# An attention block on one core: the input by tokens and the output through 32x32 squares instead of TensorE transposes

## The chip, the cores and the metric

One core of one Trainium2 chip runs the kernel. The metric is the device time of one execution in microseconds (us); lower is better.

## The reference

The input `x` has 16 batches of 256 channels and 32 x 32 positions, all in 32-bit floats. A batch is 1024 tokens of 256 channels. What is computed, batch by batch:

```python
xn = group_norm(x, 8 groups) * norm_w + norm_b
q, k, v = qkv_w @ xn + qkv_b
x1 = x + proj_w @ (softmax(q.T k / 16) v) + proj_b      # first attention, residual
t = tokens(x1)                                          # [1024, 256]
n = layer_norm(t); c = n / |n|
t = t + softmax((c c.T) ** 2) @ n                       # second attention
l = layer_norm(t)
y = (l @ (sign(w - mean(w)) * mean|w|)) + bias
t = t + round(clip(y, -1, 1) * 7) / 7                   # quantised feed-forward
out = t turned back to [256, 32, 32]
```

## The kernel before, in words

Each engine has a program written out by hand, and semaphores tie them together. A number is split into a high and a low part, and each product takes three matmuls (low by high, high by low, high by high). The weights are folded once at the start: queries and keys into one matrix, values and projection into another.

A batch has a `front` and a `back` (TensorE L532 and L604, ScalarE L724 and L764, VectorE L972 and L1031, GpSimd L1170). The front of batch b also finishes batch f = b - 1. On TensorE the order of the front is: transpose the first half of `x_raw` into `turn` (`x_by_tokens`, L372, 8 transposes of 128x128), queries 0 (12 matmuls of 512 columns), the second half of `x_raw`, queries 1, transposes of the second norm of batch f (`turn_ln2`, L507), values, the feed-forward product (`ffn`, L515, 8 matmuls of 512 columns for a half), and the transposes of `tok` of batch f (`turn_t`, L525, 8 for a half), which bring the tokens into the layout of the output. Two score blocks (`scores1`, L405) go between these. Then come steps s = 1 to 8: a score block, the transposes of the exponentials (`turn_e1`, L429) and the product with the values of the block before (`product1`, L437). After step 1 a product waits until VectorE has read the result before it out of the shared bank: `product1(b, 1)` waits for `t1_made` of `residual1(b, 0)`. Then follow the second scores (L455), and in the back the second product (L484).

VectorE works strictly in its written order: `x_tokens` (L873) adds the bias to the transposed `x` and writes `x_tok`, which `residual1` (L898) adds; `row_max` (L889), `e1T_lo` (L894, the low part of the exponentials), `gn_sums` (L851, statistics of the next batch), `clip` (L953), and `output` (L966), which adds the quantised result to the transposed `tok` in PSUM. ScalarE applies scale and bias of the feed-forward (`ffn_out`, L716), and GpSimd rounds (L1161). SyncE issues the DMAs: two loads of 512 KB for a batch (L281), once the transposes have read `x_raw` and it is normalised, and two stores of 512 KB (L285), whose runs in memory are 2 KB. The last batch runs the same steps from other PSUM banks (`LAST`, L261).

Of the kernel before, what the change touches and what calls it, by code (L numbers as in the profile page):

```python
# [30 lines left out]
ALU = mybir.AluOpType  # L31
# [4 lines left out]
BANK = 512  # L36
GROUPS = 8
# [7 lines left out]
def build(nc, x, norm_w, norm_b, qkv_w, qkv_b, proj_w, proj_b, ffn_w, ffn_b, out):  # L45
# [11 lines left out]
    assert KC == 2 and N == 2 * BANK and C // GROUPS == 32  # L57
    scale = float(C) ** -0.5

    x_d = x.rearrange("b (k p) h w -> b p k (h w)", p=P)  # L60
    out_d = out.rearrange("b (k p) h w -> b p k (h w)", p=P)

    with ExitStack() as ctx:
# [25 lines left out]
        out_bias = sb("out_bias", [P, C])  # L89
        norm_w_c = sb("norm_w_c", [P, KC])  # L90
        norm_b_c = sb("norm_b_c", [P, KC])
        ffn_b_c = sb("ffn_b_c", [P, KC])
# [8 lines left out]
        xn_lo = sb("xn_lo", [P, KC, N], F32R)  # L101
        x_tok = sb("x_tok", [P, NT, C])
# [8 lines left out]
        y_sb = sb("y_sb", [P, 2, KC, HALF])  # L111
# [52 lines left out]
        bv_wide = expo[:, 1, 0:KC * P].rearrange("p (t c) -> p t c", c=P)  # L164
        abs_w = x_tok[:, 0:KC, :]

# [28 lines left out]
        xT_up = sem("xT_up")  # L195
# [53 lines left out]
        tT_up = sem("tT_up")  # L249
        out_made = sem("out_made")  # L250
        stored = [sem("stored0"), sem("stored1")]

        QKV_LOADS, NORM_LOADS, FFN_LOADS = 16 * 3, 16 * 2, 16 * 3
# [6 lines left out]
        PLACES = dict(ln2T=[turn, turn], y=y_wide, tT=[turn, turn])  # L260
        LAST = dict(ln2T=[turn, wide[1]], y=[y_wide[0], [narrow[0][:, :], narrow[1][:, :]]], tT=[turn, wide[1]])  # L261
# [16 lines left out]
        def _(sp):  # L278
# [4 lines left out]
            def store(f, hf):  # L283
                sp.wait_ge(out_made, 2 * f + hf + 1)
                sp.dma_start(out_d[f, :, :, hf * HALF:(hf + 1) * HALF], y_sb[:, hf]).then_inc(stored[hf], 16)  # L285

            load_x(0)
            with nc.allow_non_contiguous_dma("columns of biases, once"):
# [6 lines left out]
                sp.dma_start(ffn_b_c[:, :], ffn_b.rearrange("(k p) -> p k", p=P)).then_inc(ffn_loaded, 16)  # L295
# [935 lines left out]
```

## Time and profile before

| | |
|---|---|
| Median of 3 runs | 1854.93 us (1854.73 to 1854.97) |
| The profiled execution | 1856.45 us |
| Its span, first to last instruction | 1854.7 us |
| Mean granted clock of TensorE | 0.998 |
| TensorE busy | 99% |
| VectorE, ScalarE, GpSimd busy | 68%, 49%, 52% |
| Read from memory, written to it | 18.23 MB, 16.78 MB |

All durations below are of the profiled execution, which took 1.75 us more than its span and 1.52 us more than the median. Batches repeat: the first turn of `x` of one batch starts at 1265.93 us, and the batch after it runs in the same order some 114 us later. Times in the rows are counted from the start of the span. A matmul's duration in a row includes its passage through the array, so the pace of TensorE is read from one start to the next.

### The profile page before, as it was taken

To read this page: it belongs to the slowest core of one execution; us is meant where nothing else is said; L and a number is where in the kernel's file an instruction comes from. 1 tells how busy PE (TensorE), PEld (TensorE's weight loads), DVE (VectorE), ACT (ScalarE), POOL (GpSimd) and SP (SyncE) were. 2 spreads that over 40 slices of the span, in tenths; PEclk is the share of its full clock that TensorE was granted. 3 is DMA by queue.
4 is the path that set the end of the run, shared out by engine and by line. 5 is a ranking of instruction groups with operands and counts; after the bars stand their busy time and mean duration, and the time that the engine had idled before them with its cause. 6 is when DMAs were issued, how large, how long until landed. Compare 5 with 4: busy or idle time off the path is not lost.

```text
span 1854.7 us, 36871 instructions
## 1 busy us (share of the span) xinstructions
PE 1835.7 (99%) x12834; PEld 1699.1 (92%) x12834; DVE 1268.1 (68%) x2516; ACT 906.7 (49%) x1444; POOL 959.6 (52%) x2262
## 2 busy tenths in 40 slices
PE   7999999999999999999999999999999999999997
PEld 6999999989899998999989999999998999989997
DVE  6676766767666676666767667676676766767566
ACT  3545546445463544635446354454544536355452
POOL 0654727457274472734737356372654727447272
PEclk9999999999999999999999999999999999999999
DMA  2000010000100001000010100001000010000000
GB/s 77 1 24 24 1 45 0 23 23 0 45 0 23 23 0 45 0 34 11 0 45 0 45 0 10 35 0 45 0 23 23 0 45 0 23 23 0 24 1 23
DMA packets 16415, 35.42 MB, mean 19 GB/s; under 512 B 2688, under 2 KB 4096, under 8 KB 16384
## 3 DMA queue, kind: packets, MB, share of 16 engines
q1 hardware_dynamic: 16384, 35.01, 5.2%
q8 instruction: 19, 0.31, 0.1%
q14 instruction: 12, 0.10, 0.0%
HBM read 18.23 MB, written 16.78 MB: 19 GB/s over the span
## 4 chain that ended last, share of the span: by engine, by line
PE 98%; DVE 0%; DMA 0%; ACT 0%; SPq 0%; issue 0%; POOL 0%; ACTq 0%; POOLq 0%; DVEq 0%
PE wide L322 35%; PE narrow L424 8%; PE narrow L426 8%; PE narrow L425 8%; PE turn L434 6%; PE wide L424 5%; PE wide L426 5%; PE wide L425 5%; PE narrow L322 5%; PE wide L520 3%; PE turn L481 3%; PE turn L377 2%; PE narrow L452 2%; PE turn L511 1%; PE turn L528 1%; DMA qkv_b_c<-in_L_conv_qkv_b 0%
## 5 line engine op out<-in xcount | busy, mean ns | idle before, releaser
L322 PE MATMUL wide<-xn_hi,prob 128*128 128x512 f32 x1024 | 310.1, 404 | 0.0
L676 ACT ACTIVATE prob<-turn 128x1024 fp32r<-128x1024 f32 x128 | 131.3, 1026 | 322.0 <-PE turn L434 322.0
L1109 POOL TENSOR_TENSOR ln_v<-ln_mv,ln_eps 128x1 f32<-128x1 f32 x256 | 49.3, 193 | 428.8 <-DVE ln_mv L909 251.7
L891 DVE TENSOR_REDUCE neg_max<-wide 128x1 f32<-128x1024 f32 x128 | 156.4, 1222 | 123.0 <-PE wide L322 123.0
L690 ACT ACTIVATE ln<-tok,ln_shift,ln_r 128x256 f32<-128x256 f32 x128 | 77.2, 603 | 319.7 <-POOL ln_shift L1114 319.7
L424 PE MATMUL narrow<-prob 128*128 128x256 f32 x768 | 225.0, 293 | 0.0
L426 PE MATMUL narrow<-prob 128*128 128x256 f32 x768 | 217.0, 283 | 0.0
L425 PE MATMUL narrow<-prob 128*128 128x256 f32 x768 | 216.9, 282 | 0.0
L322 PEld LDWEIGHTS wide<-xn_hi,prob 128*128 128x128 f32 x1024 | 182.8, 188 | 35.4
L896 DVE TENSOR_TENSOR prob<-turn,prob 128x1024 fp32r<-128x1024 f32 x128 | 156.7, 1224 | 61.8 <-ACT prob L676 61.8
L669 ACT ACTIVATE expo<-wide,neg_max 128x1024 f32<-128x1024 f32 x128 | 142.5, 1113 | 58.2 <-DVE neg_max L891 58.1
L322 PE MATMUL wide<-xn_lo,prob 128*128 128x512 f32 x512 | 160.7, 395 | 0.0
L1149 POOL TENSOR_TENSOR prob<-expo,prob 128x128 fp32r<-128x128 f32 (+6 forms) x112 | 150.3, 1358 | 9.0 <-DVE prob L919 9.0
L424 PE MATMUL narrow<-val,prob 128*128 128x258 f32 x512 | 148.6, 290 | 0.0
L425 PEld LDWEIGHTS narrow<-prob 128*128 128x128 f32 x768 | 147.1, 191 | 0.0
L424 PE MATMUL wide<-val,prob 128*128 128x258 f32 x512 | 146.9, 287 | 0.0
L424 PEld LDWEIGHTS narrow<-prob 128*128 128x128 f32 x768 | 146.9, 191 | 0.0
L426 PEld LDWEIGHTS narrow<-prob 128*128 128x128 f32 x768 | 146.7, 191 | 0.0
L1138 POOL TENSOR_TENSOR cos_x<-ln_x,len_i 128x256 f32<-128x256 f32 x128 | 78.7, 615 | 130.7 <-ACT ln_x L683 126.6
L426 PE MATMUL wide<-val,prob 128*128 128x258 f32 x512 | 145.0, 283 | 0.0
L426 PE MATMUL narrow<-val,prob 128*128 128x258 f32 x512 | 145.0, 283 | 0.0
L425 PE MATMUL wide<-val,prob 128*128 128x256 f32 x512 | 144.6, 282 | 0.0
(171 smaller groups left out, 5479.1 us busy)
## 6 DMA issues: line engine op xcount, KB each, us to landing
x_raw<-in_x SPq DMA_DIRECT2D x32, 512.0 KB, 3.9
out<-y_sb SPq DMA_DIRECT2D x32, 512.0 KB, 2.8
tok<-in_L_conv_qkv_w SPq DMA_DIRECT2D x1, 768.0 KB, 6.8
ln<-in_L_conv_proj_w SPq DMA_DIRECT2D x1, 256.0 KB, 6.8
ln<-in_L_ffn_weight SPq DMA_DIRECT2D x1, 256.0 KB, 3.0
out_bias<-in_L_conv_proj_b SPq DMA_DIRECT2D x1, 128.0 KB, 3.8
qkv_b_c<-in_L_conv_qkv_b SPq DMA_DIRECT2D x1, 3.0 KB, 7.4
norm_w_c<-in_L_conv_norm_w SPq DMA_DIRECT2D x1, 1.0 KB, 6.1
```

Source lines behind the costliest of these rows:

```text
L322: mm = pe.matmul(o, lhsT, r, start=first and i == 0, stop=last and i == len(parts) - 1)
L424: pe.matmul(o[:, 0:w], hi, value_hi(j), start=j == 0, stop=False)
L425: pe.matmul(o[:, 0:C], hi, value_lo(j), start=False, stop=False, skip_group_check=True)
L426: mm = pe.matmul(o[:, 0:w], lo, value_hi(j), start=False, stop=j == NT - 1)
L434: mm = pe.transpose(turn[:, tile(j)], expo[:, n % DEEP, tile(j)], ident[:, :])
L669: act.activation(expo[:, n % DEEP], wide[n % 2][:, :], ACT.Exp, bias=neg_max[:, n:n + 1], accum_out=row_sum1[:, n:n + 1]).then_inc(e1_made, 1)
L676: act.activation(eT_hi[:, n % 2], turn[:, :], ACT.Copy).then_inc(eT_hi_made, 1)
L690: act.activation(ln2[:, n], tok[:, n], ACT.Identity, bias=ln2_shift[:, n:n + 1], scale=ln2_r[:, n:n + 1]).then_inc(ln2_made, 1)
L891: dve.tensor_reduce(neg_max[:, n:n + 1], wide[n % 2][:, :], AX.X, ALU.max, negate=True).then_inc(max_made, 1)
L896: dve.tensor_sub(eT_lo[:, n % 2], turn[:, :], eT_hi[:, n % 2].bitcast(F32)).then_inc(eT_made, 1)
L1138: pool.tensor_tensor(cos_x[:, r], ln_x[:, r], len_i[:, n:n + 1].broadcast_to([P, C]), ALU.mult).then_inc(cos_made, 1)
L1149: pool.tensor_sub(prob[:, 1, J, row], expo[:, J % DEEP, row], prob[:, 0, J, row].bitcast(F32)).then_inc(p_made, 1)
```

## The change

The token layout of `x` is no longer made on TensorE. `x` is loaded a second time, in 32 DMAs for a batch (4 groups of 32 partitions by 8 channel blocks), each of 256 runs of 128 bytes, so that every 32x32 square lies in one group of 32 partitions (`x_quad`). ScalarE adds the bias to it in place, in 8 instructions of 256 elements (`bias_quad`), which stand between the instructions of `layer_norm2` of the batch before. VectorE turns the squares, in two instructions of 1024 elements (`x_tokens`), which stand in steps 0 and 2 of the front.

The feed-forward product is made with tokens on the partitions (16 matmuls of 256 columns for a half), and its scale and bias move from ScalarE to VectorE (`ffn_out`, one instruction of 1024 elements for a half). `output` stands in steps 1 and 4 now. It adds `tok` to the quantised result, both in SBUF, and turns the squares of the sum into `out_quad`, which lies in the memory of `ln2`. SyncE stores it in 32 DMAs for a batch, again of 128-byte runs, and the first `layer_norm2` of the next batch waits until all 32 have landed. `x_by_tokens` and `turn_t` are gone. The last batch is added by tokens, turned on TensorE (`turn_last`), copied out by ScalarE and VectorE, and stored in two DMAs with 2 KB runs.

The first load of the squares stands behind the loads of the weights. In the loop SyncE issues, in this order: the two loads of `x_raw` of batch b + 1, the 32 loads of squares of batch b + 1 once `x_tokens` of batch b is done, and the 32 stores of batch b - 1 once its second `output` is done.

```diff
     x_d = x.rearrange("b (k p) h w -> b p k (h w)", p=P)
+    xq_d = x.rearrange("b (cb cc) (n tq) w -> b tq cc cb n w", cc=Q, tq=P // Q)
+    outq_d = out.rearrange("b (cb cc) (n tq) w -> b tq cc cb n w", cc=Q, tq=P // Q)
     out_d = out.rearrange("b (k p) h w -> b p k (h w)", p=P)
...
+        quad_bias = sb("quad_bias", [P, C // Q, Q])
...
-        ffn_b_c = sb("ffn_b_c", [P, KC])
+        ffn_bias = sb("ffn_bias", [P, C])
...
+        x_quad = sb("x_quad", [P, C // Q, NT, Q])
...
-        y_sb = sb("y_sb", [P, 2, KC, HALF])
+        y_sb = sb("y_sb", [P, 2, HT, C])
...
+        out_last = expo[:, 0:2, :].rearrange("p h (k t) -> p h k t", k=KC)
         abs_w = x_tok[:, 0:KC, :]
+        out_quad = ln2[:, :, :].rearrange("p t c -> p (t c)").rearrange("p (cb n tt) -> p cb n tt", cb=C // Q, n=NT)
...
-        PLACES = dict(ln2T=[turn, turn], y=y_wide, tT=[turn, turn])
-        LAST = dict(ln2T=[turn, wide[1]], y=[y_wide[0], [narrow[0][:, :], narrow[1][:, :]]], tT=[turn, wide[1]])
+        PLACES = dict(ln2T=[turn, turn], y=y_wide)
+        LAST = dict(ln2T=[turn, wide[1]], sum=[turn, wide[1]], y=[y_wide[0], [narrow[0][:, :], narrow[1][:, :]]])
...
-            def store(f, hf):
-                sp.wait_ge(out_made, 2 * f + hf + 1)
-                sp.dma_start(out_d[f, :, :, hf * HALF:(hf + 1) * HALF], y_sb[:, hf]).then_inc(stored[hf], 16)
+            def load_quads(b):
+                for tq in range(P // Q):
+                    for cb in range(C // Q):
+                        sp.dma_start(x_quad[tq * Q:(tq + 1) * Q, cb], xq_d[b, tq, :, cb]).then_inc(quad_loaded, 16)
+            def store(f):
+                sp.wait_ge(out_made, 2 * f + 2)
+                for tq in range(P // Q):
+                    for cb in range(C // Q):
+                        sp.dma_start(outq_d[f, tq, :, cb], out_quad[tq * Q:(tq + 1) * Q, cb]).then_inc(stored, 16)
+            def store_last(hf):
+                sp.wait_ge(last_made[hf], 2)
+                sp.dma_start(out_d[B - 1, :, :, hf * HALF:(hf + 1) * HALF], out_last[:, hf]).then_inc(last_stored, 16)
...
+            load_quads(0)

             def reload(b):
-                sp.wait_ge(xT_up, 2 * b)
                 sp.wait_ge(xn_made, 2 * b)
                 load_x(b)

+            def reload_quads(b):
+                sp.wait_ge(xT_made, 2 * b)
+                load_quads(b)
             reload(1)
+            reload_quads(1)
             with sp.Fori(1, B - 1) as b:
                 reload(b + 1)
-                store(b - 1, 0)
-                store(b - 1, 1)
-            for f in (B - 2, B - 1):
-                store(f, 0)
-                store(f, 1)
-            sp.wait_ge(stored[0], 16 * B)
-            sp.wait_ge(stored[1], 16 * B)
+                reload_quads(b + 1)
+                store(b - 1)
+            store(B - 2)
+            for hf in range(2):
+                store_last(hf)
+            sp.wait_ge(stored, 16 * QUADS * (B - 1))
+            sp.wait_ge(last_stored, 32)
...
-            def x_by_tokens(b, g):
-                if g:
-                    pe.wait_ge(xT_made, 2 * b + 1)
-                for t in range(HT):
-                    for k in range(KC):
-                        mm = pe.transpose(turn[:, t * C + k * P:t * C + (k + 1) * P],
-                                          x_raw[:, k, tile(HT * g + t)], ident[:, :])
-                mm.then_inc(xT_up, 1)
...
             def ffn(f, hf, places=PLACES):
                 pe.wait_ge(ln2T_made, 2 * f + hf + 1)
-                for m in range(KC):
+                for t in range(HT):
+                    o = places["y"][hf][t // 2][:, t % 2 * C:(t % 2 + 1) * C]
                     for k in range(KC):
                         for part in (tokT_lo, tokT_hi):
-                            mm = pe.matmul(places["y"][hf][m], sign_w[:, k, tile(m)],
-                                           part[:, k, hf * HALF:(hf + 1) * HALF],
+                            mm = pe.matmul(o, part[:, k, tile(HT * hf + t)], sign_w[:, k, :],
                                            start=k == 0 and part is tokT_lo, stop=k == KC - 1 and part is tokT_hi)
                 mm.then_inc(y_up, 1)

-            def turn_t(f, hf, places=PLACES):
+            def turn_last(hf):
+                pe.wait_ge(sum_made, 2 * (B - 1) + hf + 1)
                 for k in range(KC):
                     for t in range(HT):
-                        mm = pe.transpose(places["tT"][hf][:, k * HALF + t * P:k * HALF + (t + 1) * P],
-                                          tok[:, HT * hf + t, tile(k)], ident[:, :])
-                mm.then_inc(tT_up, 1)
+                        mm = pe.transpose(LAST["sum"][hf][:, k * HALF + t * P:k * HALF + (t + 1) * P],
+                                          y_sb[:, hf, t, tile(k)], ident[:, :])
+                mm.then_inc(last_up, 1)
...
                     pe.wait_ge(x_loaded[k], 16 * b + 16)
                 if f is not None:
-                    pe.wait_ge(pT_made, (NT - 1) * f + NT - 1)
-                x_by_tokens(b, 0)
-                if f is not None:
                     pe.wait_ge(t2_made, NT * f + NT - 1)
                 queries(b, 0)
-                x_by_tokens(b, 1)
                 if f is not None:
                     pe.wait_ge(t2_made, NT * f + NT)
                 else:
                     pe.wait_ge(prep_dve, 8)
                 queries(b, 1)
                 if f is not None:
-                    pe.wait_ge(xT_made, 2 * b + 2)
...
+                    pe.wait_ge(pT_made, (NT - 1) * f + NT - 1)
                     turn_ln2(f, 0)
...
-                    turn_t(f, 0)
-                    pe.wait_ge(y_made, 4 * f + 2)
+                    pe.wait_ge(y_made, 2 * f + 1)
                 scores1(b, 0)
                 if f is not None:
-                    pe.wait_ge(out_made, 2 * f + 1)
-                    turn_t(f, 1)
-                    pe.wait_ge(y_made, 4 * f + 4)
+                    pe.wait_ge(y_made, 2 * f + 2)
                 scores1(b, 1)
-                if f is not None:
-                    pe.wait_ge(out_made, 2 * f + 2)
-                else:
-                    pe.wait_ge(xT_made, 2 * b + 2)
                 turn_e1(b, 0)
...
-            turn_t(f, 0, LAST)
             turn_ln2(f, 1, LAST)
             ffn(f, 1, LAST)
-            turn_t(f, 1, LAST)
+            for hf in range(2):
+                turn_last(hf)
...
+            def bias_quad(b, cb):
+                if cb == 0:
+                    act.wait_ge(quad_loaded, 16 * QUADS * (b + 1))
+                mm = act.activation(x_quad[:, cb], x_quad[:, cb], ACT.Identity, bias=quad_bias[:, cb, 0:1])
+                if cb == C // Q - 1:
+                    mm.then_inc(quad_biased, 1)
+            def layer_norm2(b, n, again=True):
                 act.wait_ge(ln2_scale, NT * b + n + 1)
+                if again and n == 0:
+                    act.wait_ge(stored, 16 * QUADS * b)
                 act.activation(ln2[:, n], tok[:, n], ACT.Identity, bias=ln2_shift[:, n:n + 1],
                                scale=ln2_r[:, n:n + 1]).then_inc(ln2_made, 1)
...
-            def ffn_out(f, hf, reuse, places=PLACES):
-                act.wait_ge(y_up, 2 * f + hf + 1)
-                if reuse:
-                    act.wait_ge(stored[hf], 16 * f)
-                for m in range(KC):
-                    act.activation(y_sb[:, hf, m], places["y"][hf][m], ACT.Identity,
-                                   bias=ffn_b_c[:, m:m + 1], scale=w_mean[:, 1:2]).then_inc(y_made, 1)
...
+                if f is None:
+                    act.wait_ge(quad_bias_made, 1)
+                    for cb in range(C // Q):
+                        bias_quad(0, cb)
...
                 for n in range(NT):
-                    layer_norm2(b, n)
+                    layer_norm2(b, n, again)
+                    if more:
+                        bias_quad(b + 1, n)
...
+                act.wait_ge(last_up, hf + 1)
+                act.activation(out_last[:, hf, 0], LAST["sum"][hf][:, 0:HALF], ACT.Copy).then_inc(last_made[hf], 1)
...
             def x_tokens(b, g):
-                dve.wait_ge(xT_up, 2 * b + g + 1)
-                dve.tensor_tensor(x_tok[:, HT * g:HT * (g + 1), :],
-                                  turn[:, :].rearrange("p (t c) -> p t c", t=HT),
-                                  out_bias[:, :].unsqueeze(1).broadcast_to([P, HT, C]), ALU.add).then_inc(xT_made, 1)
+                dve.wait_ge(quad_biased, b + 1)
+                dve.transpose(x_tok[:, HT * g:HT * (g + 1), :].rearrange("p n (cb cc) -> p n cb cc", cc=Q),
+                              x_quad[:, :, HT * g:HT * (g + 1), :].rearrange("p cb n tt -> p n cb tt")
+                              ).then_inc(xT_made, 1)
...
+            def ffn_out(f, hf, places=PLACES):
+                dve.wait_ge(y_up, 2 * f + hf + 1)
+                wholes = [wide[hf][:, :]] if places is PLACES else places["y"][hf]
+                step = HT // len(wholes)
+                for i, whole in enumerate(wholes):
+                    last = dve.scalar_tensor_tensor(
+                        y_sb[:, hf, i * step:(i + 1) * step], whole.rearrange("p (t c) -> p t c", t=step),
+                        w_mean[:, 1:2], ffn_bias[:, :].unsqueeze(1).broadcast_to([P, step, C]), ALU.mult, ALU.add)
+                last.then_inc(y_made, 1)
...
-            def output(f, hf, places=PLACES):
-                dve.wait_ge(tT_up, 2 * f + hf + 1)
+            def add_tokens(f, hf):
                 dve.wait_ge(q_made, 2 * f + hf + 1)
-                dve.tensor_tensor(y_sb[:, hf], places["tT"][hf][:, :].rearrange("p (k t) -> p k t", k=KC), y_sb[:, hf],
-                                  ALU.add).then_inc(out_made, 1)
+                dve.tensor_tensor(y_sb[:, hf], tok[:, HT * hf:HT * (hf + 1)], y_sb[:, hf], ALU.add).then_inc(sum_made, 1)
+            def output(f, hf):
+                add_tokens(f, hf)
+                dve.wait_ge(ln2T_up, 2 * f + 2)
+                dve.wait_ge(sum_made, 2 * f + hf + 1)
+                dve.transpose(out_quad[:, :, HT * hf:HT * (hf + 1)].rearrange("p cb n tt -> p n cb tt"),
+                              y_sb[:, hf].rearrange("p n (cb cc) -> p n cb cc", cc=Q)).then_inc(out_made, 1)
...
-                x_tokens(b, 0)
-                if f is None:
+                    dve.transpose(quad_bias[:, :, :], out_bias[:, :].rearrange("p (cb cc) -> p cb cc", cc=Q)
+                                  ).then_inc(quad_bias_made, 1)
                     signs()
-                x_tokens(b, 1)
...
+                    ffn_out(f, 0)
                     clip(f, 0)
...
+                    ffn_out(f, 1)
                     clip(f, 1)
...
-                    output(f, 0)
                 row_max(b, 0)
-                if f is not None:
-                    output(f, 1)
                 row_max(b, 1)
                 e1T_lo(b, 0)
+                x_tokens(b, 0)
                 if more:
                     gn_sums(b + 1, 0)
...
+                    if s == 2:
+                        x_tokens(b, 1)
+                    if f is not None and s in (1, 4):
+                        output(f, s // 4)
...
+            ffn_out(f, 0, LAST)
             clip(f, 0)
             ln2T_lo(f, 1, LAST)
             quantise(f, 0)
-            output(f, 0, LAST)
+            ffn_out(f, 1, LAST)
             clip(f, 1)
+            add_tokens(f, 0)
             quantise(f, 1)
-            output(f, 1, LAST)
+            add_tokens(f, 1)
+            for hf in range(2):
+                dve.wait_ge(last_up, hf + 1)
+                dve.tensor_copy(out_last[:, hf, 1], LAST["sum"][hf][:, HALF:N]).then_inc(last_made[hf], 1)
```

## Rows read from the trace of the kernel before

**Rows 1.** The page, parts 1 and 4: engine TensorE, and the chain by engine.

```profile
PE 1835.7 (99%) x12834; PEld 1699.1 (92%) x12834; DVE 1268.1 (68%) x2516; ACT 906.7 (49%) x1444; POOL 959.6 (52%) x2262
...
PE 98%; DVE 0%; DMA 0%; ACT 0%; SPq 0%; issue 0%; POOL 0%; ACTq 0%; POOLq 0%; DVEq 0%
```

**Rows 2.** Timeline of TensorE, start of a batch: start us, length us.

```profile
1265.93 1.03 PE L377 MATMUL turn<-ident,x_raw 128*128 128x128 f32 x8
1266.72 0.72 PE L322 MATMUL wide<-xn_hi,qk_lo 128*128 128x512 f32 x2
...
1269.61 1.03 PE L377 MATMUL turn<-ident,x_raw 128*128 128x128 f32 x8
...
1276.95 0.42 PE L520 MATMUL wide<-tokT_lo,sign_w 128*128 128x512 f32 x1
```

**Rows 3.** Timeline of TensorE, steps 1 and 2 of the same batch.

```profile
1299.15 0.64 PE L322 MATMUL wide<-xn_hi,prob 128*128 128x512 f32 x2
...
1301.95 1.04 PE L434 MATMUL turn<-ident,expo 128*128 128x128 f32 x8
1302.75 0.36 PE L424 MATMUL narrow<-prob 128*128 128x256 f32 x1
...
1305.70 0.28 PE L364 MATMUL narrow<-gn_mv,group_mean 128*128 128x2 f32 x2
```

**Rows 4.** Timeline of VectorE, where it splits the turned second norm.

```profile
1275.54 1.22 DVE L950 TENSOR_TENSOR tokT_lo<-turn,tokT_hi 128x1024 fp32r<-128x1024 f32 x1 [2.44 <-ACT tokT_hi L712]
```

**Rows 5.** Timeline of three engines after the first score block.

```profile
1288.06 1.03 PE L528 MATMUL turn<-ident,tok 128*128 128x128 f32 x8
...
1288.26 1.23 DVE L891 TENSOR_REDUCE neg_max<-wide 128x1 f32<-128x1024 f32 x1 [0.36 <-PE wide L322]
...
1290.53 0.19 ACT L669 ACTIVATION_READ_ACCUMULATOR expo<-wide,neg_max 128x1 f32 x1
```

**Rows 6.** Timeline of VectorE from the first split of exponentials to the first residual.

```profile
1293.87 1.23 DVE L896 TENSOR_TENSOR prob<-turn,prob 128x1024 fp32r<-128x1024 f32 x1 [0.70 <-ACT prob L676]
1295.01 1.28 DVE L854 BATCH_NORM_STATS2 gn_stats<-x_raw 128x6 f32<-128x512 f32 x2
...
1300.28 0.48 DVE L904 SCALAR_TENSOR_TENSOR tok<-narrow,inv_sum,x_tok 128x256 f32<-128x256 f32 x1
```

**Rows 7.** Groups of VectorE, shapes kept apart.

```profile
L924 DVE TENSOR_TENSOR prob<-expo,prob 128x512 fp32r<-128x512 f32 x32 | 82.1, 2567 | 1.1
...
L875 DVE TENSOR_TENSOR x_tok<-turn,out_bias 128x1024 f32<-128x1024 f32 x32 | 39.2, 1224 | 30.7 <-PE turn L377 30.5
...
L955 DVE TENSOR_SCALAR y_sb<-y_sb 128x1024 f32<-128x1024 f32 x32 | 22.2, 694 | 34.8 <-ACT y_sb L721 33.1
```

**Rows 8.** Groups of ScalarE, shapes kept apart.

```profile
L690 ACT ACTIVATE ln<-tok,ln_shift,ln_r 128x256 f32<-128x256 f32 x128 | 77.2, 603 | 319.7 <-POOL ln_shift L1114 319.7
```

**Rows 9.** Timeline of VectorE and TensorE in steps 4 and 5.

```profile
1317.79 1.23 DVE L896 TENSOR_TENSOR prob<-turn,prob 128x1024 fp32r<-128x1024 f32 x1 [0.37 <-ACT prob L676]
...
1323.23 0.36 PE L424 MATMUL narrow<-prob 128*128 128x256 f32 x1
```

**Rows 10.** Timeline of the SyncE queue: two loads issued.

```profile
1270.81 0.92 SPq L281 DMA_DIRECT2D x_raw<-in_x  x2
```

**Rows 11.** The page, part 3: the DMA queue of loads and stores.

```profile
q1 hardware_dynamic: 16384, 35.01, 5.2%
```

**Rows 12.** DMA view of 9.2 to 10.0 us, where bias columns load.

```profile
DMA packets 506, 0.11 MB, mean 134 GB/s; under 512 B 403, under 2 KB 506, under 8 KB 506
```

**Rows 13.** Timeline of ScalarE where the back of the batch begins.

```profile
1356.60 2.00 ACT L652 ACTIVATE xn_hi<-x_norm 128x1024 fp32r<-128x1024 f32 x2
```

**Rows 14.** Timeline at the end, TensorE and VectorE.

```profile
1843.46 0.50 PE L520 MATMUL narrow<-tokT_lo,sign_w 128*128 128x512 f32 x1 [2.41 <-DVE tokT_lo L950]
...
1850.23 1.22 DVE L969 TENSOR_TENSOR y_sb<-wide,y_sb 128x1024 f32<-128x1024 f32 x1
```

**Rows 15.** Windows, one stretch: busy of PE, PEld, DVE, ACT, POOL; clock; DMA.

```profile
1844.50:1847.50 3.00, 3.00 (x11) 2.46 (x10) 1.46 (x2) 1.01 (x2) 0.00 (x0) 0.50 0.17 66
```

More of the change, by code:

```diff
@@ L36 @@
 BANK = 512
+Q = 32
 GROUPS = 8
@@ L56, in build @@
     NP = len(PARTS)
-    assert KC == 2 and N == 2 * BANK and C // GROUPS == 32
+    assert KC == 2 and N == 2 * BANK and C // GROUPS == 32 and W == Q
     scale = float(C) ** -0.5
     x_d = x.rearrange("b (k p) h w -> b p k (h w)", p=P)
+    xq_d = x.rearrange("b (cb cc) (n tq) w -> b tq cc cb n w", cc=Q, tq=P // Q)
+    outq_d = out.rearrange("b (cb cc) (n tq) w -> b tq cc cb n w", cc=Q, tq=P // Q)
     out_d = out.rearrange("b (k p) h w -> b p k (h w)", p=P)
@@ L194, in build @@
         xn_lo_made = sem("xn_lo_made")
-        xT_up = sem("xT_up")
+        quad_loaded = sem("quad_loaded")
+        quad_bias_made = sem("quad_bias_made")
+        quad_biased = sem("quad_biased")
         xT_made = sem("xT_made")
@@ L248, in build @@
         q_made = sem("q_made")
-        tT_up = sem("tT_up")
+        sum_made = sem("sum_made")
         out_made = sem("out_made")
-        stored = [sem("stored0"), sem("stored1")]
+        stored = sem("stored")
+        last_up = sem("last_up")
+        last_made = [sem("last_made0"), sem("last_made1")]
+        last_stored = sem("last_stored")
+        QUADS = (P // Q) * (C // Q)
         QKV_LOADS, NORM_LOADS, FFN_LOADS = 16 * 3, 16 * 2, 16 * 3
@@ L714, in ln2T_hi, with front @@
                                ).then_inc(ln2T_hi_made, 1)
-            def ffn_out(f, hf, reuse, places=PLACES):
-                act.wait_ge(y_up, 2 * f + hf + 1)
-                if reuse:
-                    act.wait_ge(stored[hf], 16 * f)
-                for m in range(KC):
-                    act.activation(y_sb[:, hf, m], places["y"][hf][m], ACT.Identity,
-                                   bias=ffn_b_c[:, m:m + 1], scale=w_mean[:, 1:2]).then_inc(y_made, 1)
-            def front(b, f, more, reuse=True):
+            def front(b, f, more):
                 query_hi(b, 0)
@@ L732, in front @@
                     ln2T_hi(f, 1)
-                    ffn_out(f, 0, reuse)
                 value_hi(b, 2)
                 value_hi(b, 3)
-                if f is not None:
-                    ffn_out(f, 1, reuse)
+                if f is None:
+                    act.wait_ge(quad_bias_made, 1)
+                    for cb in range(C // Q):
+                        bias_quad(0, cb)
                 exp1(b, 0)
@@ L762, in front, with back @@
                         layer_norm1(b, NT - 1)
-            def back(b, more):
+            def back(b, more, again=True):
                 if more:
@@ L780, in _ @@
             front(0, None, True)
-            back(0, True)
-            front(1, 0, True, reuse=False)
+            back(0, True, again=False)
+            front(1, 0, True)
             with act.Fori(2, B - 1) as b:
@@ L793, in _ @@
                 layer_norm2(f, n)
-            ffn_out(f, 0, True, LAST)
             ln2T_hi(f, 1, LAST)
-            ffn_out(f, 1, True, LAST)
+            for hf in range(2):
+                act.wait_ge(last_up, hf + 1)
+                act.activation(out_last[:, hf, 0], LAST["sum"][hf][:, 0:HALF], ACT.Copy).then_inc(last_made[hf], 1)
         @block.vector
@@ L990, in front @@
                 if f is not None:
+                    ffn_out(f, 1)
                     clip(f, 1)
-                    output(f, 0)
                 row_max(b, 0)
-                if f is not None:
-                    output(f, 1)
                 row_max(b, 1)
                 e1T_lo(b, 0)
+                x_tokens(b, 0)
                 if more:
@@ L1058, in _ @@
             quantise(f, 0)
-            output(f, 0, LAST)
+            ffn_out(f, 1, LAST)
             clip(f, 1)
+            add_tokens(f, 0)
             quantise(f, 1)
-            output(f, 1, LAST)
+            add_tokens(f, 1)
+            for hf in range(2):
+                dve.wait_ge(last_up, hf + 1)
+                dve.tensor_copy(out_last[:, hf, 1], LAST["sum"][hf][:, HALF:N]).then_inc(last_made[hf], 1)
         @block.gpsimd
```

6 lines of the change are left out of this document (3 added, 3 removed).

## The prediction

> **What bounds the kernel now.** First the page: TensorE is busy 99% of the span, and the chain that ended last runs through it for 98% [rows 1]. So the first question is what leaves TensorE, and the second which wait opens once it has less to do. A busy time of matmuls includes their passage through the array, so I take the pace from starts in the timeline [rows 2, 3]. Then I read VectorE's timeline beside it, where the new instructions go [rows 6], and the places where one engine hands over to another with little to spare [rows 4, 5, 9]. All sums are made against the profiled execution of 1856.45 us, which is 1.52 us above the median; the difference is then put to the median of 1854.93 us.
>
> **TensorE loses 3.52 us a batch.** Eight turns of `x` take from 1265.93 to 1266.72, that is 0.79 us [rows 2]. The 12 query matmuls behind them take 2.89 us (1266.72 to 1269.61), while 12 of the same size behind a product take 2.80 us (1299.15 to 1301.95) [rows 2, 3]. So a group of turns is worth 0.79 + 0.09 = 0.88 us. A batch has four of them that go: two of `x`, and two of `tok`, which are the same instructions on another tile. That is 3.52 us, and it occurs in the 15 batches from 1 to 15: 52.8 us. In batch 0 only the two of `x` go, 1.76 us.
>
> The feed-forward product keeps its 4096 columns for a half. By 12 x 512 columns in 2.80 us it takes 1.87 us; by 24 x 256 columns in 2.95 us (1302.75 to 1305.70) [rows 3] it would take 1.97 us. Most of that difference is the slow first matmul behind the turns, which `ffn` hasn't got. I take nothing, and keep 0.2 us a batch (3 us in all) for the range.
>
> **VectorE gives back 1.7 us in 14 batches.** Its order is strict. Between the first split of the exponentials and the first residual it has no idle time: a 1024-element instruction starts at 1293.87 and the next one at 1295.01, so each such one is worth 1.14 us, and the residual that frees the bank ends at 1300.28 + 0.48 = 1300.76 [rows 6]. TensorE starts the product that waits for it (`product1(b, 1)`) at 1302.75 [rows 3]. The slack is 1.99 us, less the handover; one handover from VectorE to TensorE takes at most 0.19 us (an instruction from 1275.54 to 1276.76, the waiting matmul at 1276.95) [rows 2, 4]; at 0.14 us for it, 1.85 us are left. Into this stretch go `x_tokens(b, 0)` and `output(f, 0)`: a turn, an add, and a turn that waits for the add.
>
> - The add has 1024 elements, as L875 has (1224 ns) [rows 7], plus 0.04 us as the turn waits for it: 1.26 us. GpSimd waits for the residual's statistics here, so nothing of it reads SBUF beside.
> - No row shows a 32x32 turn. Below, it might cost what one-source work of 1024 elements in SBUF costs, 694 ns (L955). Above, VectorE is at its slowest where it reads SBUF beside GpSimd: 512 elements in 2567 ns (L924), so 5.13 us for 1024 [rows 7]. I take 1.14 us, the pace of ordinary work on 1024 elements, since GpSimd is idle here.
>
> Together 1.14 + 1.26 + 1.14 = 3.54 us, less 1.85: a stall of 1.7 us at `product1(b, 1)`. It needs both an old output to finish and statistics of the next batch to make: batches 1 to 14, so 14 x 1.7 = 23.8 us. In batch 0 there is no output, and in batch 15 no statistics; the slack holds there.
>
> The Trainium skill (Vector Engine (DVE) Microarchitecture Reference, 3.8) says that the turning array sustains one element per cycle per lane; no run so far shows it. By it the price would be that of the ordinary rows, and the sum the same.
>
> **Step 4.** The second `output` stands behind the split that starts at 1317.79. VectorE is free at 1318.93, and the next product waits until 1323.23 [rows 9]. Less 0.64 us for the reciprocal and the residual and 0.15 for the handover, 3.5 us are open. It needs 1.26 + 1.14 = 2.4 us. GpSimd has two jobs of 256 elements in SBUF then; if the add were contended throughout it would take 5.13 us [rows 7], a stall of 2.8 us. I take one more microsecond, 3.4 us in all, which just fits: no stall.
>
> **The front.** VectorE loses two `x_tokens` (1.22 us each) and two `output` adds, and gains two `ffn_out` of 1024 elements from PSUM, which is L875's form [rows 7]: no more than before. Where the cover shrinks is the first softmax row: TensorE is through with score block 0 at 1288.06, VectorE starts its maximum at 1288.26, and ScalarE has the sum read out at 1290.72 [rows 5]. That is 2.66 us, plus up to 0.19 for the handover. Before, turns and a score block covered it; now only a score block of 2.80 us. It fits by 0.1 us at best and misses by 0.05. The split of the second norm [rows 4] is covered by the values as before. For such near misses I take 0.1 us in each of 15 batches: 1.5 us.
>
> **ScalarE.** The eight `bias_quad` cost 603 ns each by L690, and ScalarE idles 319.7 / 128 = 2.5 us before each of these norms [rows 8]. Cover: the product of the back. In batch 0 there is no such cover: 8 x 0.6 = 4.8 us stand before the first exponential, so of the 1.76 us saved there I keep 0.6 (bounds: all of it, or 3 us lost).
>
> **DMAs.** A batch gets 32 loads and 32 stores, on a queue where two issues take 0.92 us [rows 10]: 64 x 0.46 = 29.4 us. Their runs are 64 x 256 = 16384 packets, 1024 for each of 16 engines. Below, a packet costs 25 ns: 506 in 0.8 us where bias columns load [rows 12]. Above, 94 ns: 5.2% of 16 x 1854.7 us for 16384 packets of 2 and 4 KB or less [rows 11]. So 26 to 96 us. They may start after step 2 (about 1306) and must have landed when the first norm of the back may start, behind the two ScalarE instructions that end at 1358.60 [rows 13]: 52 us. Queued behind that norm are all the others and the next queries' copies. A 128-byte run is nearer to the bias columns, so I take it as hidden; the order of the queue does not delay `x_raw`, which has a whole batch.
>
> The Trainium skill (DMA: Bandwidth & Descriptors, Specifications) speaks against the change: under 512 bytes a transfer falls short of line rate and is read, modified and written. If that were to decide, it is the last rival below; no row shows a 128-byte store.
>
> **The end.** Now the last half is finished by an ending at 1850.23 + 1.22 = 1851.45 [rows 14]. The new order puts behind the last product the other half's add (1.14), a turn (0.79 at full clock, 1.6 at half) and a copy of 512 elements (0.7), with two handovers: 2.9 to 3.7 us more. I take 3.2.
>
> **Sum.** -52.8 - 0.6 + 23.8 + 1.5 + 3.2 = -24.9 us. The profiled execution would take 1831.5 us, the median 1830.0 us. A measurement of this kernel can tell 0.2% (3.7 us) from no change.
>
> **Rivals.**
> 1. *The turn is cheap, or the stall doesn't come.* At 0.65 us a turn the stall is 2.56 - 1.85 = 0.7 us, so 14 us less: 1816; with no stall 1806. For it: L955 works on the same bytes faster. Against: few rows are that fast. 12%.
> 2. *TensorE's clock falls at each stall.* At the end TensorE idles 2.41 us before 1843.46 [rows 14], and then the granted clock is 0.50 for 3 us [rows 15], the lower level of 1.2 GHz. Three microseconds at half lose 1.5 us of work; 14 times is 21 us more: 1851. Against: my stall is shorter than that idle time, with full work on both sides. 12%.
> 3. *Many small handovers come to light.* With TensorE 3.5 us shorter, each 0.04 to 0.3 us of slack may turn out missing; 1 us a batch is 15 us: 1845. 9%.
> 4. *Slower: a turn costs two passes.* Place: the same stall. At a turn of price P it is 2P - 0.6 us a batch, and the change loses from P = 2.1 us on (14 x 3.6 = 50). At 2.3 us it is 4.0 us, 56 in all, and step 4 then misses by 1.1 us, another 16: 24.9 us of gain become 23 of loss, 1878. For it: no row shows this instruction, and L924 shows that work in SBUF can be far dearer. 12%.
> 5. *Slower: the 128-byte runs are late.* Above 51 ns a packet (some 60 with ScalarE's idle time) the first norm waits for the stores and TensorE behind it. At 94 ns they need 96 us and miss by over 35 us in each batch: 2300. 5%.
>
> The forecast has 50%, with 1822 to 1841 as its own range. That the change doesn't do what it says has no chance of its own: every removed turn is in the code of the loop.
>
> **Numbers.** 80% range: from rival 1's middle to past rival 2, 1808 to 1860. Faster by over 0.2% (under 1851.2): 50 + 12 + 9 and half of rival 2, with a little of 4: 78%. Within 0.2%: 6%. Slower: 16%.
>
> **What would show it.** Right: no turn of `x_raw` or `tok` on TensorE; a batch of about 112.2 us instead of 114; one idle time of TensorE of 1.7 us a batch, before the second product of the values, released by the residual; the turns near 1.2 us; the first norm of the back not waiting for a DMA. Wrong: turns of 2 us or more, a granted clock under 1.00 in steps 2 and 3, idle time before the feed-forward or the first turn of exponentials, or ScalarE waiting on `stored` or `quad_loaded`.

## The result: slower, 1930.05 against 1854.92 us

| | before | after |
|---|---|---|
| median of 4 runs, us | 1854.92 (1854.73 to 1854.97) | 1930.05 (1927.35 to 1933.26) |
| ratio, 95% interval | 1 | 1.0406 (1.0388 to 1.0424) |
| profiled execution, span | 1856.45, 1854.7 | 1930.54, 1928.8 |

The forecast was 1830.0 us with a range to 1860; the time is 100 us above it.

The page of the changed kernel, parts 1 and 4 (as [rows 1]), part 3 (the DMA queues) and part 6 (issues):

```profile
PE 1823.0 (95%) x12594; PEld 1692.2 (88%) x12594; DVE 1340.4 (69%) x2583; ACT 916.0 (47%) x1510; POOL 963.8 (50%) x2262
...
q1 hardware_dynamic: 277920, 51.98, 13.9%
q8 instruction: 136, 2.23, 0.5%
...
PE 75%; DVE 8%; issue 7%; POOL 7%; SPq 1%; ACT 1%; POOLq 0%; DMA 0%; DVEq 0%; ACTq 0%
...
x_quad<-in_x SPq DMA_DIRECT2D x512, 32.0 KB, 2.3
out<-ln SPq DMA_DIRECT2D x480, 32.0 KB, 1.9
```

TensorE no longer fills the chain, and "issue" has 7% of it: time in which the engine waited for nothing that the profile shows. One line looked harmless. The instruction queue, q8, brought 136 packets of 16 KB. Before the change it brought 19:

```profile
q8 instruction: 19, 0.31, 0.1%
```

Where does TensorE wait now? Its waits in the changed kernel (engine, line, releaser: us in total, times, longest):

```profile
PE narrow L445 <- issue: 44.4, 18, 3.6
PE narrow L445 <- POOL prob L1189: 21.1, 8, 2.8
PE narrow L445 <- DVE tok L920: 19.5, 14, 1.4
```

The third is the stall that was forecast, 14 times. The other two are 26 idle times, two for each of the 13 times that the loop returns to its head (its body runs 14 times). A turn of the loop is one pass through its body here; the turns of `x` and of the squares are transposes. The timeline of TensorE shows them for one turn, at the first instructions of the loop body, `product2(f, 0)`:

```profile
1293.08 0.82 PE L502 MATMUL turn<-ident,expo 128*128 128x128 f32 x6
1296.61 0.38 PE L445 MATMUL narrow<-val,prob 128*128 128x258 f32 x1 [2.71 <-POOL prob L1189]
...
1297.68 0.34 PE L447 MATMUL narrow<-val,prob 128*128 128x258 f32 x1
1299.86 0.58 PE L445 MATMUL narrow<-val,prob 128*128 128x258 f32 x1 [1.84 <-issue]
```

Nine matmuls run between the two idle times. The clock follows; windows of the same turn, with the granted clock third from the end:

```profile
1297.00:1297.50 0.50, 0.50 (x6) 0.50 (x6) 0.47 (x2) 0.00 (x0) 0.50 (x1) 1.00 0.00 0
...
1297.60:1304.40 6.80, 4.96 (x25) 4.69 (x24) 4.73 (x6) 0.00 (x0) 3.37 (x2) 0.51 0.48 155
```

So for 6.8 us, the second idle time among them, the granted clock is at the lower of its two levels, 1.2 GHz. TensorE is busy for 4.96 us of these, and half of that, about 2.5 us, is lost. With 2.71 + 1.84 us of idle time that is 7.0 us in this turn. A turn of the loop takes 119.41 us (the forecast stall stands at 1240.56 and again at 1359.97).

### The profile page after: what moved, and what is told of

It reads as the page before. It is cut to its first block, busy times and chain, and to the rows that moved or that the text cites. A ratio compares the mean times of both kernels' runs of the same rounds, so it can differ in the third digit from the quotient of the medians.

```text
span 1928.8 us, 39117 instructions
## 1 busy us (share of the span) xinstructions
PE 1823.0 (95%) x12594; PEld 1692.2 (88%) x12594; DVE 1340.4 (69%) x2583; ACT 916.0 (47%) x1510; POOL 963.8 (50%) x2262
## 3 DMA queue, kind: packets, MB, share of 16 engines
q1 hardware_dynamic: 277920, 51.98, 13.9%
## 4 chain that ended last, share of the span: by engine, by line
PE 75%; DVE 8%; issue 7%; POOL 7%; SPq 1%; ACT 1%; POOLq 0%; DMA 0%; DVEq 0%; ACTq 0%
PE wide L352 22%; PE narrow L445 8%; PE narrow L447 8%; PE narrow L446 8%; POOL prob L1189 5%; PE wide L445 5%; PE wide L447 5%; PE wide L446 5%; PE turn L455 5%; PE narrow L352 4%; PE wide L542 3%; DVE gn_stats L870 2%; PE turn L532 1%; SPq L299 1%; PE turn L502 1%
## 5 line engine op out<-in xcount | busy, mean ns | idle before, releaser
L352 PE MATMUL wide<-xn_hi,prob 128*128 128x512 f32 x1024 | 305.3, 402 | 0.0
L445 PE MATMUL narrow<-val,prob 128*128 128x258 f32 x512 | 162.8, 318 | 65.5 <-issue 44.4
L445 PEld LDWEIGHTS narrow<-val,prob 128*128 128x128 f32 x512 | 111.0, 217 | 72.2 <-issue 48.9
L445 PEld LDWEIGHTS narrow<-prob 128*128 128x128 f32 x768 | 146.7, 191 | 22.8 <-DVE tok L920 22.8
L447 PE MATMUL narrow<-val,prob 128*128 128x258 f32 x512 | 158.1, 309 | 0.0
L446 PE MATMUL narrow<-val,prob 128*128 128x256 f32 x512 | 157.9, 308 | 0.0
L1189 POOL TENSOR_TENSOR prob<-expo,prob 128x128 fp32r<-128x128 f32 (+6 forms) x112 | 149.9, 1354 | 9.0 <-DVE prob L935 9.0
```

What stands on the lines that cost most here:

```text
L352: mm = pe.matmul(o, lhsT, r, start=first and i == 0, stop=last and i == len(parts) - 1)
L445: pe.matmul(o[:, 0:w], hi, value_hi(j), start=j == 0, stop=False)
L446: pe.matmul(o[:, 0:C], hi, value_lo(j), start=False, stop=False, skip_group_check=True)
L447: mm = pe.matmul(o[:, 0:w], lo, value_hi(j), start=False, stop=j == NT - 1)
L1189: pool.tensor_sub(prob[:, 1, J, row], expo[:, J % DEEP, row], prob[:, 0, J, row].bitcast(F32)).then_inc(p_made, 1)
```

## The experiments

Three theories were set against each other. **A, the instruction fetch:** TensorE's code comes from memory in blocks, packets of 16 KB on q8. While the body of the loop is resident (all of it held by the engine), a turn fetches nothing; now the body lies differently against these blocks, and is fetched anew in every turn. **B, the traffic:** the 64 transfers of 128-byte runs per batch delay the fetches or push code out. **C, the engines:** VectorE's new work makes GpSimd's `e2_lo` late, as the releaser "POOL prob L1189" suggests.

TensorE's program was counted for this, a matmul as two instructions (weight load and multiply). Ahead of the loop the changed kernel has 33 fewer than before (16 turns of `x` in batch 0, and a wait); the body has 1658, against 1693. A block is taken as 256 instructions; idle78 and idle82 test that.

**idle17, idle100: the body moved.** Idle transposes go where TensorE has nothing to do; their result is overwritten:

```diff
             pe.wait_ge(consts_made, 3)
+            for _ in range(17):
+                pe.transpose(turn[:, 0:P], ident[:, :], ident[:, :])
             group_means(0)
```

> This is the kernel after the change, with 17 transposes of the identity (34 instructions for TensorE) added ahead of its first group mean, where TensorE has nothing to do before 7 us. They restore nearly the number of TensorE instructions (1187 against 1154) that stood ahead of the loop before the change. Theory A (the instruction fetch: in the changed kernel TensorE's loop body lies so against the 16 KB blocks in which its code is fetched that it no longer stays resident, and every turn of the loop fetches it again): the 16 KB fetches fall from 136 to about 20, none of them in the loop after its first pass; the two stalls of TensorE at the start of product 2 (about 2.7 and 1.9 us) and the stretch at clock 0.50 behind them go; time 1815 to 1836 us. Theory B (the 64 transfers of 128-byte runs per batch delay the fetches): nothing changes, 1928 to 1933 us, 136 fetches. Theory C (VectorE's added work makes GpSimd's e2_lo late at product 2): nothing changes, 1928 to 1933 us.

Measured: 1832.85 us (1832.47 to 1833.31), ratio to before 0.9869 (0.9853 to 0.9886). 34 instructions that compute nothing save 97 us. The instruction queue has 19 packets again. The waits of TensorE in idle17, the first two:

```profile
PE narrow L445 <- DVE tok L922: 19.5, 14, 1.4
PE turn L550 <- DVE y_sb L996: 3.4, 1, 3.4
```

The DMA view from 1230 to 1700 us, a stretch with four heads of the body. First the changed kernel, nine fetches a turn, then idle17, where the two are of the code behind the loop:

```profile
q8 instruction: 36, 0.59, 0.5%
```

```profile
q8 instruction: 2, 0.03, 0.0%
```

Traffic, engines and their order are unchanged, and both kinds of stall are gone, also the one named after GpSimd. B and C fall for this kernel; A stands.

> The kernel after the change with 100 such idle transposes (200 instructions) instead of 17: a control for the idle transposes themselves. Theory A: the place of the loop against the blocks is what counts and not the number of idle transposes; 200 instructions move it on into a place where the body (some 1658 instructions, 6.5 blocks of 256) again touches 8 blocks: about 130 fetches, 1920 to 1940 us. If instead any idle work at the start helps, 1815 to 1836 us. Theories B and C: 1928 to 1935 us.

Measured: 1880.65 us (1870.34 to 1890.04), 92 fetches. Slower than idle17 by 48 us and faster than expected. Some 6 us of this lie ahead of the loop: the first forecast stall ends at 166.05 us, against 160.33 in idle17. The trace has 8 idle times of 2.4 to 4.3 us at the head of the body, and so 5 turns of 13 without one. The waits of TensorE:

```profile
PE narrow L445 <- issue: 23.7, 6, 4.3
...
PE narrow L445 <- POOL prob L1191: 5.1, 2, 2.6
```

So it isn't idle work that helps. But the expectation of 1920 us and more missed: with 8 blocks touched, a turn may still be spared.

**before60: the same illness in the old kernel.** The same edit with 60 transposes, in the kernel before.

> The kernel before the change with 60 idle transposes (120 instructions) ahead of TensorE's first group mean and nothing else. Theory A: its loop body (1693 instructions, 6.6 blocks) is moved onto 8 blocks, and the old kernel gets the same illness: 110 to 140 fetches instead of 19, a stall of some 3 to 5 us at the start of product 2 and a stretch at clock 0.50 each turn, 1930 to 1975 us. Theories B and C: 1855 to 1857 us, since neither the transfers nor VectorE are touched.

Measured: 1906.59 us (1904.29 to 1915.1), ratio 1.0281 (1.0256 to 1.0306), 137 fetches. The trace shows one idle time in each turn, for instance:

```profile
1273.54 0.82 PE L481 MATMUL turn<-ident,expo 128*128 128x128 f32 x6
1277.17 0.38 PE L424 MATMUL narrow<-val,prob 128*128 128x258 f32 x1 [2.81 <-issue]
1277.39 0.28 PE L425 MATMUL narrow<-val,prob 128*128 128x256 f32 x1
```

The cause doesn't need the change. The price is below the expected one: 50 us, 3.8 per turn, since there is one idle time a turn and the clock falls in only 7 of 13.

**beforequads: the traffic alone.** In the kernel before, on SP's queue:

```diff
             with sp.Fori(1, B - 1) as b:
                 reload(b + 1)
+                sp.wait_ge(xT_made, 2 * b + 2)
+                sp.wait_ge(quad_loaded, 16 * 32 * (2 * b - 1))
+                load_quads(b + 1)
                 store(b - 1, 0)
                 store(b - 1, 1)
+                sp.wait_ge(quad_loaded, 16 * 32 * (2 * b))
+                load_quads(b + 1)
```

> The kernel before the change with 64 loads of 128-byte runs per loop turn added on SP's queue (the quad loads of x, twice), into a buffer that nothing reads; TensorE's and VectorE's code is untouched. Theory B (this traffic delays the instruction fetches or throws the code out): stalls at the start of product 2 and over 100 fetches of 16 KB, 1900 to 1940 us. Theory A: 19 to 25 fetches and 1854 to 1860 us; so too theory C.

Measured: 1856.29 us, ratio 0.9995 (0.9986 to 1.0005), with all the packets:

```profile
q1 hardware_dynamic: 268800, 65.48, 15.9%
q8 instruction: 19, 0.31, 0.1%
```

B falls here too. The added transfers were loads; 128-byte stores were not added to the kernel before. They run in idle17, though, as in the changed kernel, and there nothing is fetched again.

**idle60, idle8: the same number in the other kernel, and a smaller one.** The edit of idle17 with 60 and with 8.

> The kernel after the change with the same 60 idle transposes (120 instructions) that made the kernel before slower by 50 us. By the instruction fetch the shorter body (1658 against 1693 instructions) still fits onto 7 blocks of 256 there: 1832 to 1835 us and about 19 fetches of 16 KB. If what counts is only whether there are few or many idle transposes, or if idle work at the start does harm by itself, it is slow like idle100 and before60: over 1870 us.

Measured: 1834.88 us (1832.95 to 1836.1), 20 fetches. The 60 transposes that cost the kernel before 50 us take 95 us off the changed one.

> The kernel after the change with only 8 idle transposes (16 instructions). The body then begins 16 instructions further on. If its last instructions just reach into an eighth block in the changed kernel, a few are enough: 1831 to 1836 us; if 16 are too few, still over 1900 us and more than 100 fetches. Either way it places the edge between 0 and 34 instructions.

Measured: 1936.71 us (2 runs), 136 fetches. The edge lies between 15 and 33 instructions. The timeline places it better. Here three matmuls run between the two idle times, where the changed kernel has nine:

```profile
1297.91 0.38 PE L445 MATMUL narrow<-val,prob 128*128 128x258 f32 x1 [2.65 <-POOL prob L1191]
1298.13 0.28 PE L446 MATMUL narrow<-val,prob 128*128 128x256 f32 x1
1298.25 0.28 PE L447 MATMUL narrow<-val,prob 128*128 128x258 f32 x1
1300.93 0.58 PE L445 MATMUL narrow<-val,prob 128*128 128x258 f32 x1 [2.39 <-issue]
```

Six matmuls fewer, with a register instruction for every three, are 14 instructions, and the body was moved by 15. So the second idle time stands at a fixed place in the code, the end of a block, some 25 instructions into the changed kernel's body. The next four runs test it.

**idle12, idle14, idle78, idle82: both edges.**

> The kernel after the change with 12 idle transposes. In its trace TensorE stops for the second time behind the 9th matmul of the loop body, and in idle8 (15 instructions more ahead of the body, since one wait melts into another instruction) behind the 3rd: by the program's order a block of code ends there, some 25 instructions into the body of the changed kernel. 12 idle transposes move the body on by 23 instructions, so it still begins one to three before the end of a block and touches 8: over 1900 us, more than 100 fetches. If the edge isn't where the blocks say, 1831 to 1837 us.

Measured: 1943.71 us (2 runs), 136 fetches. The two idle times have become one:

```profile
1305.01 0.58 PE L445 MATMUL narrow<-val,prob 128*128 128x258 f32 x1 [6.05 <-issue]
```

> The kernel after the change with 14 idle transposes, 4 instructions more than idle12: the body is moved on by 27 and begins just inside the next block, so it touches 7. 1831 to 1837 us and 19 or 20 fetches, no stall at the start of product 2. If the blocks are not the cause, the same as idle12.

Measured: 1831.92 us (1831.89 to 1831.94), 19 fetches. **Two transposes, four instructions of some 5000, are worth 112 us.** The edge lies between 23 and 27 instructions.

> The other edge. With 78 idle transposes (155 instructions) the body begins some 130 instructions into its first block; 130 + 1658 is 1788, less than 7 blocks of 256 (1792): 1831 to 1838 us and about 20 fetches.

Measured: 1837.88 us (1836.86 to 1838.89), 20 fetches, no such stall. It is 6 us above idle14, and all of that lies ahead of the loop, where the long row of idle transposes ends late: the first forecast stall ends at 165.78 us, against 159.72 in idle14, and the last at 1626.10 against 1619.81.

> 8 instructions more than idle78: 138 + 1658 is 1796, over 7 blocks of 256. The last few instructions of the body reach into an eighth block: at least some turns of the loop fetch again, over 1860 us and over 60 fetches. If seven blocks are not the limit, the same as idle78.

Measured: 1856.74 us (8 runs, 1851.95 to 1863.87), 56 fetches; it was expected above 1860 with over 60. The side of the edge is right, the price too high: in the profiled execution only four turns stall, by 4.0 to 4.2 us:

```profile
PE narrow L445 <- issue: 16.2, 4, 4.2
```

With idle100 it shows two kinds of bad place. Where the body begins just ahead of a block's end (idle8, idle12, the changed kernel) every turn fetches 9 blocks. Where its last instructions reach into an eighth block, only some turns do. before60 is of the second kind by its place, and yet fetched in every turn; why, no run shows.

**split17: the forecast stall tested.** On top of idle17:

```diff
+                    if f is not None and s == 1:
+                        add_tokens(f, 0)
-                    if f is not None and s in (1, 4):
-                        output(f, s // 4)
+                    if f is not None and s in (3, 5):
+                        output(f, s // 4, add=s == 5)
```

> The kernel after the change with the 17 idle transposes, and VectorE's first output in two pieces: the add stays in step 1 (the first residual overwrites what it reads), its turn goes from step 1 to step 3; the second output goes whole from step 4 to step 5. If the 1.39 us stall at product 1 of each batch is the price of VectorE's added work ahead of the first residual, one turn (1.25 us) less leaves 0 to 0.2 us of it: 14 x 1.2 = 17 us off 1832.85, 1813 to 1820 us, with no fetches in the loop. If the stall has another cause, or only moves to a later product, 1828 to 1836 us.

Measured: 1814.01 us (1813.75 to 1815.29), ratio 0.9769 (0.9756 to 0.9782). The listed stall is gone, and what is left shows only in the starts. TensorE in split17, then in idle17:

```profile
1156.27 1.04 PE L455 MATMUL turn<-ident,expo 128*128 128x128 f32 x8
1157.38 0.39 PE L445 MATMUL narrow<-prob 128*128 128x256 f32 x1
...
1267.31 1.04 PE L455 MATMUL turn<-ident,expo 128*128 128x128 f32 x8
1268.41 0.39 PE L445 MATMUL narrow<-prob 128*128 128x256 f32 x1
```

```profile
1168.84 1.03 PE L455 MATMUL turn<-ident,expo 128*128 128x128 f32 x8
1171.27 0.38 PE L445 MATMUL narrow<-prob 128*128 128x256 f32 x1 [1.39 <-DVE tok L922]
...
1283.60 0.38 PE L445 MATMUL narrow<-prob 128*128 128x256 f32 x1 [1.39 <-DVE tok L922]
```

From the turns to the product it takes 0.80 us in [rows 3], 1.10 us here and 2.43 us in idle17. The whole stall is thus 1.63 us, of which the waits list only 1.39, and 0.30 us are left in split17, more than the 0 to 0.2 expected.

**sums17: the rest of it.** `gn_sums(b + 1, 1)` moves on top of that from step 1 to step 2, behind the first residual.

> The split version with 17 idle transposes, and in addition the second sums of the group norm (two statistics of 512 elements and an aggregation, 1.3 us of VectorE) go from ahead of the first residual to just behind it. In the split version TensorE begins product 1 of the second tile 1.10 us after the turns of the exponentials ahead of it, against 0.80 us before the change: 0.30 us of the stall are left. VectorE works without a pause from there to the second residual, whose time doesn't move, and the product that waits for that one has about 0.8 us to spare. So only the 0.30 us should go, 14 times: 1809 to 1811 us. If the group mean, which TensorE takes up 1.4 us after the first residual, then comes late or the slack of the next product isn't there: 1813 to 1818 us.

Measured: 1809.04 us (1808.6 to 1810.93), ratio 0.9751 (0.9737 to 0.9764); the product now starts 0.79 us after its turns. This is the best version, 2.5% faster than the kernel before:

```profile
1256.80 1.04 PE L455 MATMUL turn<-ident,expo 128*128 128x128 f32 x8
1257.59 0.36 PE L445 MATMUL narrow<-prob 128*128 128x256 f32 x1
```

## Why the prediction was wrong

**The step that failed is "TensorE loses 3.52 us a batch".** It counted what the removed matmuls take, and put at nothing what their removal does to the supply of code: the turns of `x` in batch 0 stand ahead of the loop, and without them the body begins 33 instructions earlier, touches 8 blocks instead of 7, and is fetched again in each turn (136 packets on q8 instead of 19). The sum had no term for this, no rival had it, and the range stopped at 1860. The profile of before could have raised the question. Its queue q8 brought 11 of its 19 blocks in the first 230 us, none up to 1690 us, the rest behind the loop: the body stays resident, and that is a condition that an edit can break. The cost, 1930.05 - 1832.85 = 97 us, is 7.5 us in each of 13 turns, against a forecast gain of 24.9 us.

All other steps can be read in idle17, where the body is resident:

| term | forecast | measured |
|---|---|---|
| TensorE, 15 batches | 3.52 each, -52.8 | 3.28 each, -49.2 |
| stall at `product1(b, 1)`, 14 times | 1.7 each, +23.8 | 1.63 each, +22.8 |
| the end | +3.2 | +3.7 |
| batch 0 and near misses | +0.9 | -1.2 (the rest) |
| sum | -24.9 | -23.9 (spans 1854.7 and 1830.8) |

- **TensorE's gain.** A batch took 114.02 us (1265.93 [rows 2] to 1379.95) and takes 111.04 in split17 (1156.27 to 1267.31), 0.30 of it stall: 3.28. The rest of 0.24 us lies partly in the feed-forward product, whose 16 matmuls take 1.92 us a half, against 1.88 for the 8 before, and in the values, 2.91 against 2.89 (starts in the timelines). The forecast kept 0.2 us a batch aside for the former and 0.1 for small handovers. Timeline of TensorE in the kernel before, one batch behind [rows 2]:

```profile
1379.95 1.03 PE L377 MATMUL turn<-ident,x_raw 128*128 128x128 f32 x8
```

- **The turn.** 1.14 us by the pace was nearly right: it lasts 1234 and 1246 ns, close to the add's 1197, and in idle17 the next instruction starts 1.16 and 1.17 us after it (1161.88 to 1163.04, 1169.40 to 1170.57). With that rival 1 (cheap) and rival 4 (two passes) fall. Groups of VectorE in the changed kernel:

```profile
L891 DVE STREAM_TRANSPOSE x_tok<-x_quad 128x1024 f32<-128x1024 f32 x32 | 39.5, 1234 | 0.0
L994 DVE TENSOR_TENSOR y_sb<-tok,y_sb 128x1024 f32<-128x1024 f32 x32 | 38.3, 1197 | 0.0
L1001 DVE STREAM_TRANSPOSE ln<-y_sb 128x1024 f32<-128x1024 f32 x30 | 37.4, 1246 | 3.2
```

- **Step 4.** No stall, as forecast.
- **The DMAs.** Hidden, as forecast, though the issue was underpriced at 0.46 us. Eight stores take 6.37 us of SP's queue in the changed kernel, 0.80 each:

```profile
1289.55 6.37 SPq L305 DMA_DIRECT2D out<-ln  x8
```

 In idle17 the 64 issues of a batch take 23.74 + 24.43 = 48.2 us, where 29.4 were forecast and 52 were open, so less was to spare than the forecast had. They end at 1223.8 us, and the first norm of the back starts at 1234.88. A packet took 15 ns on average (14.5% of 16 x 1830.8 us for 277920 packets in idle17), less than the 25 to 94 counted. ScalarE waits once for the quads, 0.8 us in all, and never for a store. Rival 5 (late runs) falls. The Trainium skill's warning (DMA: Bandwidth & Descriptors, Specifications) about runs under 512 bytes may hold for the transfers themselves; it decided nothing here.
- **The clock.** Rival 2 had it fall at each forecast stall. In idle17 the clock stays at 1.00 behind the 1.39 us, in all 14 batches; one of the windows:

```profile
1172.00:1173.00 1.00, 1.00 (x11) 1.00 (x10) 1.00 (x2) 0.00 (x0) 0.92 (x4) 1.00 0.00 0
```

 It did fall behind idle times of the fetches, though not behind all (7 of 13 in before60), and in the turn shown above it makes up a third of the price.
- **The end.** From the first feed-forward matmul at the end to the end of the span it was 18.2 us (1836.52 to 1854.7), and is 21.8 in idle17 (1808.96 to 1830.8): 3.7 us more, against 3.2. The two rows, of the kernel before and of idle17:

```profile
1836.52 0.39 PE L520 MATMUL wide<-tokT_lo,sign_w 128*128 128x512 f32 x1
```

```profile
1808.96 0.28 PE L542 MATMUL wide<-sign_w,tokT_lo 128*128 128x256 f32 x1
```

The rivals and the chances were all about durations and waits. With the body resident the forecast sum holds to within a microsecond, and part of that is luck: TensorE's gain came out 3.6 us smaller than forecast, and the stall and the rest made up for 3.1 us of it, less 0.5 at the end. The stall, its place and its releaser were foreseen. What decided the time of the change as it stands was a term that the sum did not have.

## What to carry to other kernels

A loop whose code only just stays resident on its engine is a resource of its own, and an edit that moves or shortens code can lose it. Look at the instruction queue's packets before and after: a count that grows with the turns is a refetch, and idle time at the head of the body, named "issue" or after a bystander, is its price. Count the instructions of body and preamble in blocks, and test with a few idle ones ahead of the loop before you blame the edit; here 34 idle instructions and three moved pieces of VectorE's work (two outputs and the sums) turned 4% slower into 2.5% faster.

## What the hardware showed that was not expected

- **TensorE kept a loop body of some 1690 instructions resident, and lost it by its place.** Bodies of 1658 instructions that touch 7 blocks of 256 were not fetched again (idle14, 17, 60, 78), those that touch 8 were (the changed kernel, idle8, 12, 82, 100). The count of instructions is the program's; where a block ends was read from where TensorE stops. The Trainium skill (Runtime: NRT & Kernel Launch, Instruction fetch mechanics) gives TensorE 128 KiB, 2048 instructions, in blocks of 256, filled in order, and says that a branch to code outside the window waits for a fetch. The runs agree with the block and with the wait: 1.8 and 2.7 us for two blocks one by one in the turn shown, 6.05 us in one piece in idle12. The section also puts that window at two pages; the runs do not agree with this, since seven blocks stayed resident. Why 7 blocks are the limit and not 8 isn't shown; fetching the block behind the loop's end in each turn would explain it, and would fit the 9 fetches a turn of a body that touches 8.
- **The releaser in the waits can be a bystander.** "POOL prob L1189" stood for 21.1 us of the changed kernel's idle time and for none of idle17's, with the same order on GpSimd.
- **A stall can be larger than the waits say.** 0.24 of 1.63 us showed only in the distance of two starts.
